# Clears and second weights behind the scattered rows, and the router's tables in five parts

## The reference

```
x = x + 0.5 * ffn(layernorm(x))
x = x + mamba2(layernorm(x))
x = x + 0.5 * ffn(layernorm(x))

ffn(x):   logits = x @ router_w.T                      # 8 experts
          scores, top = top_k(logits, 2)
          y_e  = (silu(x @ wg[e]) * (x @ wu[e])) @ wd[e]    # 512 -> 256 -> 512
          out  = sum over the two chosen e of scores * y_e + shared expert (with biases)
```

## Time and profile before

| | us |
|---|---|
| median of 3 runs | 2311.66 |
| the profiled execution's own time | 2313.75 |
| its span, first to last instruction | 2312.0 |
| PE busy | 2156.3 (93%) |
| DVE busy | 1474.8 (64%) |
| ACT busy | 1432.8 (62%) |
| POOL busy | 1376.3 (60%) |

### The profile page before, as it was taken

The page is one execution under the profiler, slowest core; times in us unless marked ns, Lnnn a source line. Parts: engine busy times, 40 slices in busy tenths (PEclk is TensorE's granted clock), DMA queues, the critical chain, the costliest instruction groups (busy, mean ns, idle before and its releaser), DMA issues. The chain is left out here.

```text
span 2312.0 us, 42896 instructions
## 1 busy us (share of the span) xinstructions
PE 2156.3 (93%) x11718; PEld 1744.5 (75%) x11718; DVE 1474.8 (64%) x2947; ACT 1432.8 (62%) x2960; POOL 1376.3 (60%) x1242
## 2 busy tenths in 40 slices
PE   5899996899999999999988999999999997789996
PEld 3687774688888888888767888888888885577775
DVE  6532247577777677777887777777777778732225
ACT  5133323777787778787658787778777774423331
POOL 2886351476666667666517666667666663586622
PEclk8999997899999999999999999999999998899998
DMA  9665361334334333433214434334433431555545
GB/s 345 243 189 175 115 174 42 101 111 108 106 84 119 106 101 99 119 97 93 65 49 127 110 86 126 98 98 105 113 102 88 117 85 35 186 188 164 160 142 164
DMA packets 204904, 285.32 MB, mean 123 GB/s; under 512 B 16288, under 2 KB 148458, under 8 KB 204816
## 3 DMA queue, kind: packets, MB, share of 16 engines
q1 hardware_dynamic: 185936, 219.18, 33.1%
q0 software_dynamic: 18880, 65.02, 9.3%
HBM read 225.43 MB, written 58.72 MB: 123 GB/s over the span
## 5 line engine op out<-in xcount | busy, mean ns | idle before, releaser
L2057 PE MATMUL mamba_p_proj<-mamba_xt_lo,mamba_in_hi 128*128 128x512 f32 x1056 | 456.9, 433 | 1.6 <-DVE mamba_bc L1708 1.1
L1708 DVE SCALAR_TENSOR_TENSOR mamba_xs<-mamba_p_proj,mamba_taps,mamba_xs 128x511 f32<-128x511 f32 (+2 forms) x384 | 285.8, 744 | 258.9 <-ACT mamba_xs L1455 250.0
L2059 PE MATMUL mamba_p_proj<-mamba_xt_hi,mamba_in_lo 128*128 128x512 f32 x1056 | 416.2, 394 | 0.0
L2058 PE MATMUL mamba_p_proj<-mamba_xt_hi,mamba_in_hi 128*128 128x512 f32 x1056 | 414.0, 392 | 0.0
L1328 POOL TENSOR_TENSOR mamba_xend<-mamba_xdt,mamba_to_end_g 128x512 f32<-128x512 f32 x128 | 134.0, 1047 | 340.0 <-DVE mamba_xdt L1768 282.8
L1334 POOL TENSOR_TENSOR mamba_mix<-mamba_mix,mamba_scores 128x512 f32<-128x512 f32 x256 | 326.5, 1297 | 14.2 <-ACT mamba_mix L1521 14.2
L1517 ACT ACTIVATE mamba_mix<-mamba_cum_l,mamba_cum_g 128x128 f32<-128x128 f32 x1024 | 324.7, 388 | 8.7 <-DMA mamba_cum_l<-mamba_cum_rows 3.8
L664 DVE TENSOR_TENSOR ffn_h<-ffn_p_gu,ffn_sil 128x256 f32<-128x256 f32 x110 | 46.8, 426 | 317.9 <-ACT ffn_sil L546 303.9
L546 ACT ACTIVATE ffn_sil<-ffn_p_gu 128x256 f32<-128x256 f32 x110 | 42.3, 385 | 319.4 <-PE ffn_p_gu L913 237.5
L2059 PEld LDWEIGHTS mamba_p_proj<-mamba_xt_hi,mamba_in_lo 128*128 128x128 f32 x1056 | 199.6, 189 | 46.5
L2057 PEld LDWEIGHTS mamba_p_proj<-mamba_xt_lo,mamba_in_hi 128*128 128x128 f32 x1056 | 200.7, 190 | 40.7 <-DVE mamba_bc L1708 2.0
(11 more groups left out here) (344 smaller groups left out, 5095.0 us busy)
## 6 DMA issues: line engine op xcount, KB each, us to landing
mamba_cum_l<-mamba_cum_rows SPq DMA_DIRECT2D x128, 512.0 KB, 5.3
mamba_rise<-mamba_exp_rows SPq DMA_DIRECT2D x256, 128.0 KB, 3.4
ffn_xs<-slots_in SPq DMA_DIRECT2D x78, 256.0 KB, 2.7
slots_out<-ffn_y SPq DMA_DIRECT2D x78, 256.0 KB
mamba_raw_x<-in_t SPq DMA_DIRECT2D x34, 512.0 KB, 5.5
mamba_raw_z<-in_t SPq DMA_DIRECT2D x32, 512.0 KB, 6.4
mamba_raw_out<-out_t SPq DMA_DIRECT2D x32, 512.0 KB, 4.7
slots_out<-ffn_xs SPq DMA_DIRECT2D x1, 9984.0 KB
```

The costliest lines, as they stand in the source:

```text
L1708: dve.scalar_tensor_tensor(dst[:, i:BLK], p_proj[:, ct, 0:BLK - i], tap[:, 0, j:j + 1], dst[:, i:BLK], ALU.mult, ALU.add).then_inc(s_conv, 1)
L2057: pe.matmul(bank, in_hi[:, piece, kk, :], xt_lo[:, kk, c], start=(kk == 0), stop=False)
L2058: pe.matmul(bank, in_hi[:, piece, kk, :], xt_hi[:, kk, c], start=False, stop=False)
L2059: last = pe.matmul(bank, in_lo[:, piece, kk, :], xt_hi[:, kk, c], start=False, stop=(kk == KT - 1))
```

## The change

It does three things.

1. SP waits for all 32 scatters of the phase (s_scat at 2 x T x 16) before it reads the first free row and issues the first of the eight clears. The later wait for the same semaphore stays and is then already met.
2. POOL issues scatter(1) right behind scatter(0); the three loads of the second expert's weights come behind it.
3. turns() is cut into turns_first (7 instructions, signals s_free), turns_second (5) and turns_third (9, signals s_tab); order_pairs() is cut into order_pairs (9) and share_pairs (8, signals s_sorted). They stand behind tick(1), tick(2), tick(3), tick(4) and tick(5). No instruction of them is added or left out.

```
             sp.wait_ge(s_zero, 1)
             sp.wait_ge(s_free, 1)
+            sp.wait_ge(s_scat, 2 * T * 16)
             for e in range(E):
                 row = sp.value_load(free_i[0:1, e:e + 1], min_val=0, max_val=(E * ROOM - 1) * P)
                 sp.dma_start(slots_in[bass.ds(row, P), :], xs[:, 0, :]).then_inc(s_zeroed, 16)
...
             scatter(0)
+            scatter(1)
             load_gate(2)
             load_up(2)
             load_out(2)
-            scatter(1)
...
-            def turns():
+            def turns_first():
                 step = link(dve, s_rank, 42)
...
+            def turns_second():
+                step = link(dve, s_rank, 48)
...
+            def turns_third():
+                step = link(dve, s_rank, 53)
...
+            def share_pairs():
+                step = link(dve, s_rank, 70)
...
             tick(1)
+            turns_first()
             tick(2)
-            turns()
+            turns_second()
             tick(3)
+            turns_third()
+            tick(4)
             order_pairs()
-            for g in range(4, JOBS):
+            tick(5)
+            share_pairs()
+            for g in range(6, JOBS):
                 tick(g)
```

## The result

The changed kernel takes 2350.26 us (median of 4 runs, 2349.39 to 2350.97) against 2312.29 us (4 runs, 2310.14 to 2315.39): ratio 1.0163, 95% interval 1.0145 to 1.0181. The forecast of 2328.5 us had the direction and less than half of the size; the range, up to 2342, doesn't hold it. The span is 2349.0 us, the mean granted clock 0.962, PE busy 2159.8 us (92%). PE is busy 3.5 us more; the rest of the 37 us is idle time.

What follows compares the result with a forecast made beforehand. PE leads; what counts is when columns(9), a routed tile's first transposes, runs, and the clock afterwards. Later loads and half-clock restarts: 9.3 + 2.7 + 2.1 + 2.7 = 16.8 us, giving 2328.5 us; range 2309 to 2342.

Steps and rivals of the forecast that it cites:

- Scatters 2.30 us earlier: POOL's scatters: without three weight issues ahead of scatter(1), the last issue ends 2.30 us earlier, at 95.51 and 2027.64.
- First clear: SP's queue: first clear 2.66 us behind the last scatter's issue, at 98.17 and 2030.30.
- Clears paced by their issues: SP's eight clears follow each other at 1.26 us, seven steps 8.8 us, the last at 107.0 and 2039.1.
- "bytes" rival: SP's clears: bytes, not issues, space them; seven steps 4.5 instead of 8.8 us; +8.2 us, 2320; chance 0.12.
- "no difference": SP's clears: register reads run ahead, steps of 0.33 us, 2.3 instead of 8.8; leaves +3.8 us; chance 0.12.
- "faster": SP and POOL issues: full DMA rings set the pace; clear steps fall to 0.33, scatters lose gaps; -5.2 us, 2306; chance 0.13.
- From the last clear to the first load, 2.78 us: SP's queue: first routed load 2.78 us behind the last clear, at 109.8 and 2041.9.
- PE reaches columns(9) well before the gate: PE, first routed tile's transposes: without late signals PE is through inner(7) by about 95, then idles over 10 us.
- Tables gain 0: turns() and order_pairs() in parts: stall of at most 5.5 us goes, but lies ahead of columns(9), so path gain 0.
- Clock, +2.7 us a phase: PE behind columns(9): restart at half clock for about 5.5 us loses about 2.7 us in each phase, bounds 0 and 5.
- Second phase, +2.1 and +2.7: Second phase: columns(9) at 2044.5 against 2042.41, +2.1 us, and +2.7 us for the clock behind it.
- late signals stay: ACT's late signals come from full DMA engines and end when the clears have landed; about 25 us, 2337; chance 0.13.

Runs made afterwards that it cites:

- the 32 KB clears: Kernel before plus eight further clears of 16 rows each behind its 32 scatters, ahead of the first load: 2337.49 us, 1.0097.
- the wait alone: Kernel before with only SP's wait for the scatters ahead of the clears, on two punctual chips: 2324.51 us (1.0152) and 2325.26 us (1.0157).
- the order alone: Kernel before with only scatter(1) moved ahead of the second expert's weights: 2293.04 us (1.0014) on a punctual chip, 2363.12 us (1.0209) on a late one.
- the break kept: Changed kernel with the second expert's weight loads back between the two scatter runs, on a late chip: 2347.1 us, 1.013 to the kernel before.
- this set: Runs on one late chip, kernel before 2315.72 us; the whole change, unchanged, repeated there: 2350.77 us, 1.0146.
- the variant with the tables alone: Kernel before with only the tables cut into five parts, on punctual chips: 2289.6 us (1.0001) and 2289.45 us (0.9999).
- set 2: Runs on one late chip; the kernel before, unchanged, takes 2315.72 us there, and its profiled repeat 2316.98 us, 1.0004.

## Why the prediction was wrong, point by point

- **Scatters 2.30 us earlier: right.** Last issue ends at 95.42 (forecast 95.51).
- **First clear: nearly.** 99.24 instead of 98.17, 3.8 us behind the last scatter's issue instead of 2.66.
- **Clears paced by their issues: right.** 8.2 us for seven steps against 8.8. The "bytes" rival is refuted by the 32 KB clears, and no step came near the 0.33 us of the "no difference" and "faster" cases.
- **From the last clear to the first load, 2.78 us: wrong size, and one of the two steps that failed.** In the changed kernel it was 5.71 and 5.03 us, with the wait alone 6.28. The step took its 2.78 us from the second phase of the kernel before, where no weight load was issued among the last clears; here 2 MB of clears lie beside the next expert's weights. I had counted these bytes only towards the spacing, and only the second expert's. From load to use I had 2.60 us; where the load is last behind the clears it was 2.9 to 4.4. The Trainium skill (DMA: Bandwidth & Descriptors, Rules for kernel authors), cited in the prediction against this wait, fits: the early clears were free, and the late ones cost 35 us.
- **"PE reaches columns(9) well before the gate" and "punctual signals": wrong, the other step that failed.** It rests on the idea that the signals were late because the DMA engines were full. They were late at a DMA share of 0.52 (85 to 95 us), and in the order alone a pause in POOL's run of scatters decides: 1.0209 without and 0.9997 with memsets. I had costed the weights' move at 0 and named POOL's later splits as its only price, but the three weight issues were the break in which two silu's got through. In the changed kernel PE is therefore still in tick 5 when the gate opens (before, in tick 7), and needs 10.7 us from load to columns(9) instead of 2.60. On the punctual chips the step holds: with the wait alone PE stands 27.30 us ahead of columns(9).
- **What the two are worth.** Without the weights' move the prediction's terms give 16.8 + 2 x 2.3 = 21.4 us; measured, with the break kept, 31.4. The move was to win 4.6 us, and the kernel with it was 3.7 us slower by the medians (the intervals overlap). So the gate was missed by 10 us and the move by 8.3; 3 us more lie between the first measurement (+38.0) and this set (+35.1). The second step decides when columns(9) runs in this trace; with the break back the gate remains, at 117.77 instead of 123.93.
- **Tables gain 0: right on the path, but their price was missed.** Stuck behind the silence, the third part fell beside POOL's splits and took 10.0 us instead of 2.6 (74.41 to 77.05 in the variant with the tables alone). It held PE, not the load; letting POOL wait for it made the changed kernel 5 us faster by the medians of one set (the intervals overlap).
- **Clock, +2.7 us a phase: wrong here.** columns(10) follows columns(9) by 5.24 us, as before (5.33), since PE had not stood ahead of columns(9); the half clock lies ahead of it, behind the 18.50 us (0.50 in 100 to 105 us). The prediction also named the wrong idle time for the low clock of 2035 to 2040 us: the 5.51 us end at 2015.70, and 6.85 us, ahead of PE's transposes at 2034.14, come just before it. Where PE does wait for its load, the step is there: 6.5 to 8.1 us to the next columns. On the punctual chips it is there without the wait too (8.07 and 7.33 us in the variant with the tables).
- **First phase in sum.** Forecast columns(9) 112.4, measured 123.93: +1.1 at the first clear, -0.6 in the spacing, +2.9 to the load, +8.1 from load to use.
- **Second phase, +2.1 and +2.7: wrong.** columns(9) shifted by 37.6 us, of which 24.3 came from the first phase (the Mamba layer's first load 363.76 to 388.09), so 13.3 were new. Of them +2.1 were forecast. By the same terms the rest is +1.3 at the first clear, -1.0 in the spacing, +2.3 to the load and +7.8 from load to use, and the last scatter was 0.9 us later than its share. Here too the load (2069.66) was long there.
- **The rival "late signals stay"** had the right effect with the wrong cause: it let them go with the clears; they go when the scatters end (silu at 97.84, last scatter's issue at 95.42, clears not begun).

What adds up: the gate alone is worth +35 us on punctual chips and about +31 on late ones (wait and tables, the break kept). Removing the break costs 46 us on late chips by itself, but all three parts together only 35 to 38. Two reasons can be read, neither tested alone: wait and silence delay the same columns(9), and in the kernel with the order alone the uncut order_pairs() ran beside POOL's splits and kept PE idle for 9.64 us more, ahead of its transposes at 117.21. The wait alone wasn't run on a late chip, and the whole change not on a punctual one.

What stays open: why two kinds of chips, and by which path GpSimd's indirect DMAs hold a signal of PE to ScalarE, or PE's own matmuls. On the late chips some signals also pass within a run of 16 (a silu at 85.10 in the kernel before of set 2), so the pause isn't the only thing that lets them through. No version beats the kernel before.

## What to carry to other kernels

Put nothing that need not wait behind a gate that the critical path passes: eight DMAs there cost 1.2 us each in issue and, with another queue's load issued just ahead of the last one, 2 to 4 us more in landing. Read what stands between two runs of scatters on GpSimd as a part of the other engines' timing, and measure a reordering on more than one chip. Tables on few elements belong ahead of POOL's tensor work, not beside it.

## What the runs showed of the hardware that was not expected

- The same kernel takes 2289 us on two chips and 2316 to 2320 us on three; idle time to "remote" on ScalarE in the scatters' stretch, 0 us against 27.0 us in the first phase, goes with it. Most of the difference does not lie there: between two profiles with columns(9) of the first phase at 102.86 in both, 18.2 of 22.1 us lie behind columns(9) in the two phases, where gathers run.
- On the late chips a run of 32 indirect DMAs without a break keeps PE's signals from ScalarE for 25.8 to 29.8 us in one piece in the first phase (four kernels), in two of them at half-full DMA engines (share 0.51 to 0.54); with 2.3 us of GpSimd memsets in the middle two silu's got through there.
- VectorE instructions on 39 elements, 0.16 to 0.39 us by themselves, take 1.7 to 2.6 us beside GpSimd's 128x1024 tensor operations, and each long row ends about when POOL's row does (102.36 and 102.34; 104.85 and 104.81; 110.28 and 110.25). The Trainium skill (SBUF — State Buffer, Who interferes with whom) says that the two engines share one pair of ports, and that for some VectorE forms, tensor_scalar and cast in a two-port mode among them, whoever issues first holds it for the whole instruction while the other waits; a tensor_tensor with two SBUF inputs contends too. The trace agrees in that these rows end with POOL's. One of them began 0.61 us ahead of POOL's and still ended with it (105.31 to 107.90, against 105.92 to 107.83), which issue order does not explain.
- Behind the scatters, DMAs whose place is read from a register follow each other on SP at 1.1 to 1.5 us, 1.2 on average, with 32 KB as with 256 KB. The load that waits for 256 KB clears goes 5.0 to 6.6 us behind the last one where another queue's 512 KB load was issued 0.6 to 2.5 us ahead of it, and 2.80 us where that load led by 0.03.
